# A gated attention and feed-forward layer on one core: the order of the work around its weight sums, its attention chain, its turn and its paired groups

## The reference

```python
def _L0_xattn_ref(x, k, v, Wh, wg_w, wo_w, gn_gamma, gn_beta):
    ...
    Q = jnp.einsum('bshd,hde->bshe', xh, Wh)
    K = jnp.einsum('bshd,hde->bshe', kh, Wh)
    V = jnp.einsum('bshd,hde->bshe', vh, Wh)
    scores = jnp.einsum('bshe,bthe->bhst', Q, K) / jnp.sqrt(jnp.float32(hd))
    masked = scores * Dn[None, :, :, :]
    A = jnp.maximum(jnp.abs(masked.sum(axis=0)), 1.0)      # summed over the batches
    O = jnp.einsum('hst,bthe->bshe', A, V).reshape(b, s, dim)
    Y = (O - mu) / jnp.sqrt(var + GN_EPS) * gn_gamma + gn_beta
    W = jax.nn.relu(x @ wg_w)
    return W * Y @ wo_w
def _L0_ffn_ref(x, gate_w, up_w, down_w, gate_s, up_s, down_s):
    ...
    g = jnp.einsum('th,ih->ti', xf, gate_w) * gate_s
    u = jnp.einsum('th,ih->ti', xf, up_w) * up_s
    hdn = jax.nn.silu(g) * u
    out = jnp.einsum('ti,hi->th', hdn, down_w) * down_s
x = x + tanh(g_xattn[0]) * _L0_xattn_ref(_layernorm(x), ctx_2048, ctx_2048, ...)
x = x + tanh(g_ffn[0]) * _L0_ffn_ref(_layernorm(x), ...)
```

## Time and profile before

| what | value |
|---|---|
| median of 3 timed runs | 1614.41 us (1611.93 to 1615.26) |
| the profiled execution's own time | 1608.08 us |
| its span, first to last instruction | 1606.3 us |
| TensorE busy, weight loads busy | 1521.7 us (95%), 1267.7 us (79%) |
| VectorE, GpSimd, ScalarE busy | 1019.7, 761.0, 681.3 us |
| mean granted TensorE clock | 0.986 |
| data moved | 305.93 MB, 190 GB/s over the span |

### The profile page before, as it was taken

How to read it: one execution, slowest core, us unless ns; L and a number is a source line. 1 busy time by engine, 2 the same in 40 slices (tenths; PEclk the granted TensorE clock), 3 DMA queues, 4 the chain that set the end, 5 groups by cost and what they waited for, 6 DMA issues and landing times.

```text
span 1606.3 us, 20329 instructions
## 1 busy us (share of the span) xinstructions
PE 1521.7 (95%) x7226; PEld 1267.7 (79%) x7226; DVE 1019.7 (63%) x1468; ACT 681.3 (42%) x1067; POOL 761.0 (47%) x804
## 2 busy tenths in 40 slices
PE   6999899898889999999999999998999999999999
PEld 5888787786777877787778878777788787887887
DVE  7677667774545556565556656543667868768672
ACT  3444343344444543545346454523344344344342
POOL 4556557651353554546355553523325426337235
PEclk9999999999899999999999999999999999999999
DMA  6888777765587777667676767674374273472332
GB/s 229 268 275 262 264 242 244 235 225 176 165 260 207 223 195 225 183 182 223 173 211 194 209 193 215 197 183 130 110 213 142 85 221 106 134 203 99 119 118 80
DMA packets 374598, 305.93 MB, mean 190 GB/s; under 512 B 258336, under 2 KB 284320, under 8 KB 374304
## 3 DMA queue, kind: packets, MB, share of 16 engines
q1 hardware_dynamic: 374496, 304.61, 63.7%
HBM read 200.23 MB, written 117.31 MB: 198 GB/s over the span
## 4 chain that ended last, share of the span: by engine, by line
PE 62%; DVE 9%; ACT 8%; DMA 7%; POOL 6%; issue 5%; SPq 4%; DVEq 0%; ACTq 0%; POOLq 0%
PE ps L1645 22%; PE pyb L1543 12%; PE po L1645 7%; PE ps L1578 5%; PE ptb L1543 4%; PE ptb L1645 3%; PE pyb L1645 3%; PE po L1543 3%; ACT turned L667 3%; POOL wyt L1428 2%; SPq L429 2%; DMA wy_scratch<-misc 2%; DMA v_scratch<-tmp 2%; ACT xn L697 2%; POOL reg L1465 1%
## 5 line engine op out<-in xcount | busy, mean ns | idle before, releaser
L1373 POOL TENSOR_SCALAR rs<-mv 128x1 f32<-128x1 f32 (+1 forms) x132 | 37.2, 282 | 386.6 <-DVE mv L1029 179.4
L1543 PE MATMUL pyb<-reg,xreg 128*128 128x512 f32 x720 | 182.4, 403 | 0.7 <-DVE xreg L942 0.7
L1645 PE MATMUL ps<-reg,gate 128*128 128x512 f32 x704 | 177.8, 395 | 4.6 <-DVE reg L1052 3.2
L1645 PE MATMUL ps<-reg,up 128*128 128x512 f32 x704 | 175.0, 391 | 0.0
L1645 PE MATMUL ps<-op,wbuf 128*128 128x512 f32 x704 | 173.9, 389 | 0.0
L1465 POOL TENSOR_TENSOR reg<-tmp,reg 128x512 fp32r<-128x512 f32 x88 | 121.5, 1381 | 109.9 <-ACT reg L716 109.9
L1645 PE MATMUL ps<-xreg,reg 128*128 128x512 f32 x704 | 163.4, 390 | 1.3 <-DVE tmp L1164 1.3
L1449 POOL TENSOR_TENSOR p5b<-p5b,p1b 128x512 f32<-128x512 f32 x44 | 56.9, 1294 | 215.3 <-ACT p5b L740 215.3
L1645 PEld LDWEIGHTS ps<-reg,gate 128*128 128x128 f32 x704 | 132.9, 191 | 32.0 <-DVE reg L1052 3.4
L1460 POOL TENSOR_TENSOR hsp<-hall,hsp 128x640 fp32r<-128x640 f32 (+2 forms) x72 | 135.8, 1902 | 46.0 <-ACT hsp L767 45.8
L1543 PEld LDWEIGHTS pyb<-reg,xreg 128*128 128x128 f32 x720 | 134.6, 192 | 28.2 <-DVE xreg L942 1.1
(11 more groups left out here) (148 smaller groups left out, 2834.7 us busy)
## 6 DMA issues: line engine op xcount, KB each, us to landing
wbuf<-ws_scratch SPq DMA_DIRECT2D x44, 896.0 KB, 4.8
xr<-in_x SPq DMA_DIRECT2D x63, 512.0 KB, 5.1
raw<-in_ctx_t SPq DMA_DIRECT2D x32, 512.0 KB, 4.8
w_scratch<-tmp SPq DMA_DIRECT2D x64, 256.0 KB, 5.0
...
```

Of the source, the lines that this page charges most:

```text
L1373: e.tensor_scalar(dst, var, eps, None, ALU.add).then_inc(s["eps"])
L1543: last = e.matmul(dst, lhs[a], rhs[b], start=(k == 0 and i == 0), stop=(k == n - 1 and i == 2))
L1645: last = e.matmul(dst, l, r, start=(k == 0 and i == 0), stop=(k == n - 1 and i == 1), skip_group_check=sums)
```

## The change

No arithmetic is changed. Five things move:

1. **Weight sums.** GpSimd's `weight_sums` pauses in group 9 (units 2 and 3 come one group later). `sums_store` moves from the head of groups 7, 9, 11, 13 to the end of groups 7, 9, 12, 14. VectorE's `low_sums` parts are spread, one at each place, over groups 7 to 10 and 12 to 13, with four in 14.
2. **The chain.** From `y_in` on, pieces move one step later (`y_in` 4, `w_load` 5, `x_again` and the affine 6, `wy_pair_mul` and `wy_pair_hi` 7, `wo_mm`, `x1`, `rstd2_pair` 9, `norm2_pair` 10, `x2_blocks` 11, `x2_out` 12); `y_out` stays at 3 and `wy_pair_lo` at 7. `v_pair_lo` moves ahead of `hidden_lo` and of the other pieces on GpSimd. The copies of weights (`weights_copy`, six DMAs in steps 5 to 7 of group 0) go one by one to step 14 of groups 1 to 6.
3. **The turn.** `w(LATE + 3)` moves ahead of the first `wo_mm`; `y_stats(2)` and `(3)`, `v_hi(2)`, `v_lo(2)`, `y_affine(3)` and `x1(0)` come earlier; `o(2)` moves ahead of `x2_t(3)`.
4. **V of pair 3.** It goes into the buffer of pair 1 (`vs_first`), so its split no longer waits for `o(2)`; pair 3 starts at step 0 instead of 1, and `v_load(4)` is issued at the turn, ahead of the load of the down weights.
5. **Paired groups.** `prepare_beside` has at most two products beside a tile only at tiles 3 and 5; `combine(m, 3)` and `operand_lo(m, 6)` move behind the last tile, into step 0 of the next group.

```diff
 def first_step(q):
-    return 7 * (q - 3) // 2 + 1 if q > 2 else -2
+    return 7 * (q - 3) // 2 + 1 if q > 3 else 2 * q - 6
...
         def vs_of(p):
-            return vs_first if p == 1 else vs_later
+            return vs_first if p in (1, 3) else vs_later
...
             for g in range(NG):
-                if g in (7, 9, 11, 13):
-                    sums_store((g - 7) // 2)
...
                 w_store(4 * g + (2 if g < NG - 2 else 1))
+                if g in (7, 9, 12, 14):
+                    sums_store((7, 9, 12, 14).index(g))
...
             v_load(3)
+            v_load(4)
...
-                    if g == 0 and 5 <= step < 8:
-                        weights_copy((G1, G2, U2)[step - 5])
+                    if 1 <= g <= 6 and step == 14:
+                        weights_copy((G1, G2, U2)[(g - 1) // 2], (g - 1) % 2)
                     for q, piece in pieces(15 * g + step):
-                        if piece == 11:
+                        if piece == 12:
                             x2_out(q)
                             x1_store(q)
                         if piece == 3:
                             y_out(q)
-                            y_in(q)
-                        if piece == 2 and q + 2 < B // 2:
+                        if piece == 2 and 2 < q < B // 2 - 2:
                             v_load(q + 2)
                         if piece == 4:
+                            y_in(q)
+                        if piece == 5:
                             w_load(q)
-                        if piece == 5:
+                        if piece == 6:
                             x_again(q)
...
             def v_hi(q):
-                    p.wait_ge("o", 1 if q == 2 else q)
+                    p.wait_ge("o", q - 1 if q < 4 else q)
...
             def hidden_hi(m):
                 p.wait_ge("h", m + 1)
+                if m == 2:
+                    p.wait_ge("o", 4)
...
             y_normal(3)
+            w_out(LATE + 3)
             y_affine(2)
+            y_affine(3)
             wy_hi(2)
-            y_affine(3)
+            v_hi(2)
             wy_hi(3)
-            v_hi(2)
...
-                if g in (7, 9, 11, 13):
-                    low_sums((g - 7) // 2, 0)
-                    low_sums((g - 7) // 2, 1)
+                if g in (7, 8, 9, 10, 12, 13, 14):
+                    low_sums(*((0, 0), (0, 2), (1, 0), (1, 2), (2, 0), (2, 2), (3, 0))[(7, 8, 9, 10, 12, 13, 14).index(g)])
+                if g == 14:
+                    low_sums(3, 1)
...
             wo_lo(3)
+            y_stats(2)
+            y_stats(3)
             wy_mul(0)
...
             for g in range(NS):
                 for step in range(15):
+                    for q, piece in pieces(15 * g + step):
+                        if piece == 1 and q + 1 < B // 2:
+                            v_pair_lo(q + 1)
                     if 1 <= step <= 11:
                         hidden_lo(11 * g + step - 1)
...
                         if piece == 7:
                             wy_pair_lo(q)
-                        if piece == 8:
+                        if piece == 9:
                             rstd2_pair(q)
```

102 lines of the change are left out of this document (50 added, 52 removed).

## The result

The changed kernel takes 1560.09 us (median of 4 runs, 1559.05 to 1563.06) beside 1614.68 us for the kernel before on the same chip: a ratio of 0.9668, 95% interval 0.9651 to 0.9685. The forecast was 1551 us, its range 1543 to 1576. Terms 1 and 4 came within a microsecond, the turn gave 3 us less than forecast, and the largest term, the chain of pairs, gave about half of what it was to give, for a wait that neither the sum nor a rival had.

A forecast was written before the change was run, and what follows sets the result against it. TensorE is busy 95% of the span, so only its gaps and slow-clock stretches can be won. 19.3 + 9.9 + 27.7 + 6.8 = 63.7 us off 1608.1 gives 1544.4, times 1.0039: 1551 us, range 1543 to 1576.

The forecast's parts named there:

- Term 1: Late groups of the first half: moved stores and spread checks of the weight sums gain 19.3 us, 12 to 20.8.
- the sums only move their burst: Rival, chance 0.08: group 8 meets the same three transfers and waits as before; 10 us less gained, 1561.
- Term 2: The turn between the halves: reordered work and earlier loads gain 9.9 us, 3 at the least, 15 at the most.
- the wait and its slow part go: At `wo_mm(2)` in the turn: the 4.16 us wait and the half-clock product behind it vanish, 5.8 us.
- Term 3: The twenty-eight pairs after the turn: the longer chain and new order gain 27.7 us, 12 to 31.
- The 0.2 us on even pairs: Wait for `wy_pair_lo` before `wo_mm`, forecast to remain on 14 even pairs, 2.8 us in all.
- I leave 2.8 + 2.5: In the pairs' stage: the loss forecast to remain, in us, of 27.3 + 5.7 = 33.0.
- Term 4: Paired groups: with less work beside down tiles, three waits for `finish` go; 6.8 us gained, 5 at the least.
- The chain was not as tight as before: Rival, chance 0.17: the chain stays as tight, even pairs again wait 1.2 us; 14 us less gained, 1565.
- The queue did eat into the turn: Rival, chance 0.13: the last store stands whole in front (3.3 us), down weights ahead of `y_out` cost 3 to 4; 1558.
- Ring order: At the turn: the whole store ahead of the loads, 5.1 us, would make the sum 3.3 us worse.
- The queue was nearly empty there: At the turn: reason for taking the loads behind the store of unit 3 only 1.8 us late.

The follow-up runs named there:

- experiment 1: The kernel before with only the weight-sums part (stores at the end of groups 7, 9, 12, 14, checks spread): 1589.7 us, ratio 0.9872.
- experiment 7: The changed kernel with the load of the down weights ahead of `v_load(4)` on SyncE: 1558.7 us, ratio 0.9693.
- experiments 3 to 5: Changed kernel, each group's last `hidden_lo` ahead of `v_pair_lo`: 0.9645; changed kernel, `v_pair_lo` at its old place: 0.9657; kernel before, `v_pair_lo` first: 0.9961.
- experiment 10: The changed kernel with `wy_pair_mul` ahead of `x2_pair_lo` at step 11 on VectorE: 1555.03 us, ratio 0.9641.
- experiment 4: The changed kernel with `v_pair_lo` back at its old place on GpSimd, behind `hidden_lo`: 1556.66 us, ratio 0.9657.
- experiment 6: The changed kernel with the six copies of weights back in steps 5 to 7 of group 0: 1570.23 us, ratio 0.9735.
- Experiment 2: The kernel before with only the paired-groups part (at most two products beside a down tile): 1600.87 us, ratio 0.9937.

## Why the prediction was right, and where it was not

**Term 1, weight sums: right.** Forecast was V's store of group 8 landing near 203.3 and ScalarE 1.8 us late for it. In the changed kernel SyncE, then ScalarE:

```profile
189.09 0.43 SPq L389 DMA_DIRECT2D ws_scratch<-sums  x1
...
197.34 0.32 SPq L311 DMA_DIRECT2D v_scratch<-tmp  x1
...
203.12 0.59 ACT L628 COPY tmp<-ps 128x512 f32<-128x512 f32 x1 [1.86 <-DMA v_scratch<-tmp]
```

It landed at 203.0 and ScalarE waited 1.86 us, under which TensorE waited for nothing. The rival that the sums only move their burst is out, and experiment 1 gives the part to itself.

**Term 2, the turn: right mechanisms, 3.0 us too large.** The first `wo_mm` was 2.2 us late (1.8 forecast), the last `x2_t` ended 18.9 us behind it (17.7), the wait before `o(3)` was 7.44 (7.5), step 0 ended 22.5 us earlier than before, 2.9 of them from this term (4.1 forecast). The rest of the miss, 1.8, is the step "the wait and its slow part go": `wo_mm(2)` still waited 2.23 us. `y_in(2)` came at 414.4, which is 432.8 less the 19.3 of term 1 and 0.9 late, but W of pair 2 landed at 424.3 behind it and held `wy_pair_mul(2)`. And that product then took 3.24 us, where the same product took 1.18 at 832.85, beside a `v_pair_lo` that had begun 0.24 us before it:

```profile
424.41 3.24 DVE L1017 TENSOR_TENSOR raw<-raw,turned 128x1024 f32<-128x1024 f32 x1 [1.81 <-DMA raw<-w_scratch]
...
424.17 2.39 POOL L1433 TENSOR_TENSOR reg<-raw,reg 128x1024 fp32r<-128x1024 f32 x1 [2.10 <-ACT reg L646]
```

In experiment 7 the same product went at 423.68 and took 1.22 us. One cause that the prediction put elsewhere: the last releaser of `o(3)` was not VectorE's statistics alone but V's split, behind `y_rstd_pair(2)` on GpSimd. The bytes behind `v_load(4)` were priced well (16.2 us to `y_in(2)`, measured 15.9). What the prediction didn't ask is how long SyncE would stand at `v_load(4)`: 15.6 us, 11 of them with no byte moving (the last row of the windows), so that `y_out(2)` landed 8 us later than need be (experiment 7).

**Term 3, the chain: the failed step.** The 0.2 us on even pairs were 0.17 to 0.18, on nine pairs. "I leave 2.8 + 2.5" was wrong: 15.3 us of idle time were left beside some 6 of slow clock. The missing wait is on work that isn't in the chain at all. The prediction moved `v_pair_lo` ahead of `hidden_lo` and followed only the one that gained; it moved `wy_pair_hi` into the step of `wy_pair_lo` and asked only when `wy_pair_lo` would be done, not who stands behind it on GpSimd. That is `hidden_lo` of the eleventh step, and the downs wait for it: 5.17 and 3.92 us, and some 4 us lost at half clock with them (experiments 3 to 5). The second part, 1.64 and 3.03 us at pair 22, comes from SyncE, which stood 11.2 us at `y_in(22)` for a turned tile that was still being read; 5.1 us were gained there when the tile came free sooner (experiment 10). In the longer chain the product that frees the tile is one step later; that this length makes the wait is read from the order, no run shows it by itself. Two more sentences of this term didn't hold as reasons. That the order of `v_pair_lo` removes the wait before `o(20)` is true, but the longer chain does it without (experiment 4). That the copies "cost about 3 us of queue each; the chain has that slack" missed their sign: with the longer chain, that they left group 0 is worth 11 us (experiment 6).

**Term 4, paired groups: right.** 7.7 for 6.8, in three steps of 2.6 us, where the waits were 2.25 to 2.27; the 0.3 us more at each I can't place. Experiment 2 gives the part to itself.

**The rivals.** The chain was not as tight as before, since the even pairs' wait went. The queue did eat into the turn, by some 2 us where that rival had 6 to 7. Ring order, which by the Trainium skill ("DMA: Bandwidth & Descriptors", section on queues, rings and completion order) would put the last store whole in front, made the first `wo_mm` 2.2 us late and not 5.1. The windows from the store (in the kernel before, from the load that stands there) to V's second load, before and now, give a reason:

```profile
358.90:372.00 13.10, 12.32 (x76) 10.91 (x75) 6.30 (x9) 5.89 (x10) 0.00 (x0) 1.00 0.74 241
339.30:353.00 13.70, 12.92 (x79) 11.42 (x78) 7.69 (x11) 5.85 (x10) 0.09 (x1) 1.00 0.96 325
```

"The queue was nearly empty there" was wrong: before, the DMA engines were busy for 0.74 of that time, in the changed kernel for 0.96. The store went into the 3.4 us that were idle (0.26 x 13.1); by that estimate 5.1 - 3.4 = 1.7 us of it are left to delay the loads. The time lay between the rivals' times for a reason that none of them gave.
